# A two-layer vision tower on one core: token weights, the routing table, class tokens and the output in another form

## What is computed

```python
# layer 0: 8 experts of width 768, top 2, gelu
top_p, top_i = jax.lax.top_k(jax.nn.softmax(x @ w_gate), 2)
h = jax.nn.gelu(take(h_all, top_i), approximate=True)   # h_all = x @ w_fc, by expert
o = sum over the 2 chosen of (h @ w_proj[expert]) * top_p / sum(top_p)
# layer 1: 16 experts, 8 of width 128 and 8 of width 256, top 8
```

## Time and profile before

| | |
|---|---|
| median of three runs | 331.63 us |
| the profiled execution | 332.05 us |
| its span, first to last instruction | 329.9 us |
| TensorE busy | 290.9 us, 88% |
| VectorE busy | 263.9 us, 80% |
| ScalarE busy | 211.1 us, 64% |
| mean granted TensorE clock | 0.938 |

### The profile page before, as it was taken

The page is one execution under the profiler, slowest core; times in us unless marked ns, Lnnn a source line. Parts: engine busy times, 40 slices in busy tenths (PEclk is TensorE's granted clock), DMA queues, the critical chain, the costliest instruction groups (busy, mean ns, idle before and its releaser), DMA issues.

```text
span 329.9 us, 6328 instructions
## 1 busy us (share of the span) xinstructions
PE 290.9 (88%) x2375; PEld 264.4 (80%) x2375; DVE 263.9 (80%) x782; ACT 211.1 (64%) x519; POOL 13.7 (4%) x38
## 2 busy tenths in 40 slices
PE   8989999999999999999979126199797999999994
PEld 6979769999999999999958014178575599999993
DVE  0347778999998989998877899889859779999962
ACT  1055477777686667777658398787051788888860
POOL 0340000000000000000010002300000000000000
PEclk9999999999999999999999555589969999999999
DMA  7990403503150504020000000002300026433402
GB/s 238 284 315 25 169 3 93 207 0 150 52 200 2 201 0 170 5 108 0 2 1 3 0 0 2 0 0 87 138 2 0 2 72 209 147 124 126 118 3 50
DMA packets 10542, 27.29 MB, mean 83 GB/s; under 512 B 1352, under 2 KB 2184, under 8 KB 10512
## 3 DMA queue, kind: packets, MB, share of 16 engines
q1 hardware_dynamic: 9776, 26.01, 23.8%
q0 software_dynamic: 416, 0.68, 0.7%
q10 hardware_dynamic: 320, 0.20, 0.3%
HBM read 26.43 MB, written 0.45 MB: 81 GB/s over the span
## 4 chain that ended last, share of the span: by engine, by line
DVE 40%; PE 33%; ACT 16%; issue 5%; DMA 3%; SPq 2%; DVEq 0%; ACTq 0%
PE bank L648 11%; ACT hid_hi L1114 7%; DVE hid_lo L1474 7%; PE bank L628 5%; DVE hidden_area L1469 5%; DVE fc_lo L1448 4%; DVE pj_parts L1451 4%; PE bank L717 4%; DMA score_area<-w_l_dram 3%; ACT pj_parts L1092 3%; PE bank L618 3%; PE bank L700 2%; PE bank L698 2%; PE bank L678 1%; DVE score_area L1761 1%
## 5 line engine op out<-in xcount | busy, mean ns | idle before, releaser
L1114 ACT ACTIVATE hid_hi<-hidden_area 128x260 fp32r<-128x260 f32 x144 | 56.3, 422 | 33.5 <-DVE hidden_area L1469 31.3
L648 PE MATMUL bank<-hid_hi,pj_parts 128*128 128x260 f32 x288 | 76.3, 286 | 0.1
L1474 DVE TENSOR_TENSOR hid_lo<-hidden_area,hid_hi 128x260 fp32r<-128x260 f32 x144 | 57.0, 427 | 9.7 <-ACT hid_hi L1114 0.6
L648 PEld LDWEIGHTS bank<-hid_hi,pj_parts 128*128 128x128 f32 x288 | 54.1, 188 | 1.1 <-DVE hid_lo L1474 0.5
L1107 ACT ACTIVATE hidden_area<-bank 128x260 f32<-128x260 f32 x144 | 49.0, 377 | 6.4 <-PE bank L700 5.6
L618 PE MATMUL bank<-zeros 128*128 128x260 bf16 x239 | 34.8, 300 | 8.3 <-ACT hidden_area L1259 6.4
L648 PE MATMUL bank<-xt_hi,fc_hi 128*128 128x260 f32 x144 | 41.2, 286 | 0.3
L700 PE MATMUL bank<-xt_lo,fc_lo 128*128 128x260 f32 x144 | 41.4, 288 | 0.0
L717 PE MATMUL bank<-hid_hi,pj_parts 128*128 128x260 f32 x144 | 40.7, 283 | 0.0
L648 PE MATMUL bank<-hid_lo,pj_parts 128*128 128x260 f32 x144 | 40.7, 282 | 0.0
L648 PE MATMUL bank<-xt_lo,fc_hi 128*128 128x260 f32 x144 | 40.7, 282 | 0.0
(11 more groups left out here) (297 smaller groups left out, 557.1 us busy)
## 6 DMA issues: line engine op xcount, KB each, us to landing
raw_area<-fc_dram SPq DMA_DIRECT2D x8, 768.0 KB, 4.4
raw_area<-pj_dram SPq DMA_DIRECT2D x8, 576.0 KB, 5.6
xn<-comb_dram SPq DMA_DIRECT2D x12, 260.0 KB, 3.8
raw_area<-fc_dram SPq DMA_DIRECT2D x6, 512.0 KB, 4.1
embed_area<-embed_in_dram SPq DMA_DIRECT2D x8, 352.0 KB, 6.7
hidden_area<-comb_dram SPq DMA_DIRECT2D x9, 260.0 KB, 4.0
raw_area<-pj_dram SPq DMA_DIRECT2D x6, 384.0 KB, 4.4
score_area<-w_l_dram SPq DMA_DIRECT2D x1, 576.0 KB, 10.4
```

Of the source, the lines that this page charges most:

```text
L648: mm = pe.matmul(out, lhs[a], rhs[b], start=start and n == 0, stop=stop and n == 2, skip_group_check=True)
L1114: act.activation(hid_hi[:, x % 3, tok], hid_w[:, x % 2, tok], ACT.Copy).then_inc(hid_hi_ready[y], 1)
L1474: dve.tensor_tensor(hid_lo[:, x % 3, tok], hid_w[:, x % 2, tok], hid_hi[:, x % 3, tok].bitcast(F32), ALU.subtract).then_inc(hid_lo_ready[y ...
```

## The change

- `weights` turns the broadcast column with a transpose in place of a matmul with the identity, tile by tile, and turns tile 2 whole for both halves; its readers take their 260 columns from column 4n of the bank. The broadcast in `statistics` becomes a transpose as well.
- In layer 0 the routing table is turned in an entry of its own, `("c", 0)`, behind tile 2's entry and ahead of tile 3's, in a pair of entry banks. ScalarE copies it behind tile 2's gelu. Projection 0 no longer waits for it, and SP's write to DRAM waits for the entry. Layer 1 keeps its place. `AHEAD` of load 1 falls from 3 to 2.
- In attention 1's head the tiles are turned in the order 0, 1, 4, 2, 3; high and low parts follow that order; the first group waits for tiles 0, 1 and 4 alone; 8 fillers in place of 16.
- `patches_out` writes a tile, two images from 128 partitions: tiles 0 and 2 from SP, 1 and 3 from ScalarE's queue.

```diff
+def turn_order(r):
+    return (0, 1, 4, 2, 3) if r == 2 else (0, 1, 2, 3, 4)
...
+TURNED_TILES = [(0, 1, 2), (2, 3, 4)]
...
+        if x == 2 and not ENTRIES:
+            order += [("c", 0)]
-    return order[at - 1:at + 1] if order[at - 1][0] == "w" else order[at:at + 1]
+    first = at if order[at - 1][0] == "h" else at - 1
+    return order[first:at + 1]
...
-AHEAD = {1: 3, E0 + 1: 2}
+AHEAD = {1: 2, E0 + 1: 2}
...
-def patches_out(queue, b, done):
-    lo = (b % 2) * PATCH
-    queue.dma_start(t["out"][b, 1:S, :], h[lo:lo + PATCH, b // 2, :]).then_inc(done, 16)
+def patches_out(queue, i, done):
+    queue.dma_start(t["out"][2 * i:2 * i + 2, 1:S, :], h[:, i, :]).then_inc(done, 16)
...
-        sp.wait_ge(comb_t_ready, 2 * (y + 1))
+        if y == 0:
+            sp.wait_ge(entry_out[0], 2 * ENTRIES[0].index(("c", 0)) + 2)
+        else:
+            sp.wait_ge(comb_t_done, 2)
...
             load1(turn // 2 + 1)
-    for b in (0, 1, 4, 5):
-        sp.wait_ge(h_done, 4 + b // 4)
-        patches_out(sp, b, out_done)
+    for i in (0, 2):
+        sp.wait_ge(h_done, 4 + i // 2)
+        patches_out(sp, i, out_done)
     sp.dma_start(t["out"][:, 0, :], h[0:B, 4, :]).then_inc(out_done, 16)
-    sp.wait_ge(out_done, 16 * 5)
-    sp.wait_ge(out_done_act, 16 * 4)
+    sp.wait_ge(out_done, 16 * 3)
+    sp.wait_ge(out_done_act, 16 * 2)
...
-        for i in range(NT):
+        for i in turn_order(r):
-            pe.wait_ge(done, of * (r + r // 2) + (i // 2 + 1) * (1 + r % 2))
+            at = [k for k in turn_order(r) if k % 2 == i % 2].index(i)
+            pe.wait_ge(done, of * (r + r // 2) + (at + 1) * (1 + r % 2))
...
-            e = tiles[first_tile(y, turn)].expert
-            for i in (0, 1, 2) if n == 0 else (2, 3, 4):
-                lo, hi = max(n * HALF, i * 128), min((n + 1) * HALF, i * 128 + rows(i))
-                mm = pe.matmul(out[:, lo - n * HALF:hi - n * HALF],
-                               (comb0, comb1)[y][0:rows(i), i, e:e + 1].broadcast_to([rows(i), 128]),
-                               ident[0:rows(i), lo - i * 128:hi - i * 128], start=True, stop=True)
-            return mm
+            e, at = tiles[first_tile(y, turn)].expert, 2 * 128 * n
+            for i in TURNED_TILES[n]:
+                last = pe.transpose(out[:, i * 128 - at:i * 128 - at + rows(i)],
+                                    (comb0, comb1)[y][0:rows(i), i, e:e + 1].broadcast_to([rows(i), 128]),
+                                    ident[0:rows(i), 0:rows(i)])
+            return last
...
                     pe.wait_ge(entry_out[y], 2 * k - 3 + n)
-                out, tok = PB[PAIRS[k % 2][n]][:, 0:HALF], slice(n * HALF, (n + 1) * HALF)
+                bank, tok = PB[PAIRS[k % 2][n]], slice(n * HALF, (n + 1) * HALF)
+                out = bank[:, 0:HALF]
                 if kind == "w":
-                    mm = weights(out, x, n)
+                    mm = weights(bank, x, n)
+                elif kind == "c":
+                    for i in ((0, 1), (2, 3, 4))[n]:
+                        mm = pe.transpose(bank[0:n_exp, i * 128 - 256 * n:i * 128 - 256 * n + rows(i)],
+                                          comb0[0:rows(i), i, :], ident[0:rows(i), 0:rows(i)])
...
             if x == 0:
-                pe.wait_ge(comb_t_ready, 2 * (y + 1))
+                pe.wait_ge(first_w_ready, 2 * (y + 1))
+            if x == 0 and y:
+                pe.wait_ge(comb_t_done, 2)
...
             weights(PB[SUMS[2 + n]], 0, n).then_inc(first_w_mm, 1)
-        comb_turn(y, n_exp)
+        if y:
+            comb_turn(y, n_exp)
...
-        pe.matmul(PB[7][:, 0:n], red[0:n, r:r + 1].broadcast_to([n, 128]), ident[0:n, 0:n],
-                  start=True, stop=True).then_inc(stat_b, 1)
+        pe.transpose(PB[7][:, 0:n], red[0:n, r:r + 1].broadcast_to([n, 128]), ident[0:n, 0:n]).then_inc(stat_b, 1)
...
     transpose_x(2)
-    fill(16)
-    wait_split_x(2)
+    fill(8)
             g = 2 * j + n
+            if g == 0:
+                pe.wait_ge(xhi_ready, 3 + 4)
+                pe.wait_ge(xlo_ready, 2 + 4)
+            if g == 1:
+                wait_split_x(2)
...
         if r == 2:
-            for i in (0, 2):
-                act.wait_ge(xt_mm, NT * r + i + 2)
-                for j in range(KC):
-                    act.activation(patches_of(xt_hi, j, i), turned_patches(j, i), ACT.Copy).then_inc(xhi_ready, 1)
+            for j in range(KC):
+                act.activation(patches_of(xt_hi, j, 0), turned_patches(j, 0), ACT.Copy).then_inc(xhi_ready, 1)
+            act.wait_ge(xt_mm, NT * r + 3)
+            for j in range(KC):
+                act.activation(cls_cols(xt_hi[0:DC, j, :]), turned_cls(j), ACT.Copy).then_inc(xhi_ready, 1)
             for j in range(KC):
-                act.activation(cls_cols(xt_hi[0:DC, j, :]), turned_cls(j), ACT.Copy).then_inc(xhi_ready, 1)
+                act.activation(patches_of(xt_hi, j, 2), turned_patches(j, 2), ACT.Copy).then_inc(xhi_ready, 1)
...
                 if kind == "w":
-                    act.activation(tok_w[x % 4][:, tok], src, ACT.Identity).then_inc(entry_out[y], 1)
+                    act.activation(tok_w[x % 4][:, tok], PB[PAIRS[k % 2][n]][:, 4 * n:4 * n + HALF],
+                                   ACT.Identity).then_inc(entry_out[y], 1)
+                elif kind == "c":
+                    tok = ((0, 256), (256, 520))[n]
+                    act.activation(comb_t[0:E0, tok[0]:tok[1]], PB[PAIRS[k % 2][n]][0:E0, 0:tok[1] - tok[0]],
+                                   ACT.Copy).then_inc(entry_out[y], 1)
...
                 act.wait_ge(first_w_mm, 2 * y + n + 1)
-                act.activation(tok_w[0][:, n * HALF:(n + 1) * HALF], PB[SUMS[2 + n]][:, 0:HALF],
+                act.activation(tok_w[0][:, n * HALF:(n + 1) * HALF], PB[SUMS[2 + n]][:, 4 * n:4 * n + HALF],
         hi_part(0)
-        comb_turned(y, (E0, E1)[y])
+        if y:
+            comb_turned(E1)
...
                 entry("w", tiles[x].turn)
+            if x == 2 and y == 0:
+                entry("c", 0)
-    def comb_turned(layer, n_exp):
-        act.wait_ge(comb_mm, layer + 1)
-        act.activation(comb_t[0:n_exp, 0:512], PB[2][0:n_exp, :], ACT.Copy).then_inc(comb_t_ready, 1)
-        act.activation(comb_t[0:n_exp, 512:520], PB[3][0:n_exp, 0:B], ACT.Copy).then_inc(comb_t_ready, 1)
+    def comb_turned(n_exp):
+        act.wait_ge(comb_mm, 1)
+        act.activation(comb_t[0:n_exp, 0:512], PB[2][0:n_exp, :], ACT.Copy).then_inc(comb_t_done, 1)
+        act.activation(comb_t[0:n_exp, 512:520], PB[3][0:n_exp, 0:B], ACT.Copy).then_inc(comb_t_done, 1)
...
-    for b in (2, 3, 6, 7):
-        act.wait_ge(h_done, 4 + b // 4)
-        patches_out(act, b, out_done_act)
+    for i in (1, 3):
+        act.wait_ge(h_done, 4 + i // 2)
+        patches_out(act, i, out_done_act)
...
-        for i in (0, 2, 4):
+        for i in turn_order(r):
+            if i % 2:
+                continue
...
-        for i in (0, 2):
-            dve.wait_ge(xhi_ready, 3 + i + 2)
+        def patches_lo(i):
                                   patches_of(xt_hi, j, i).bitcast(F32), ALU.subtract).then_inc(xlo_ready, 1)
-        dve.wait_ge(xhi_ready, 9)
+        dve.wait_ge(xhi_ready, 3 + 2)
+        patches_lo(0)
+        dve.wait_ge(xhi_ready, 3 + 4)
                               ALU.subtract).then_inc(xlo_ready, 1)
+        dve.wait_ge(xhi_ready, 3 + 6)
+        patches_lo(2)
```

More of the change, by code:

```diff
@@ L274, in build @@
         comb_mm = sem("comb_mm")
-        comb_t_ready = sem("comb_t_ready")
+        comb_t_done = sem("comb_t_done")
         xhi_ready = sem("xhi_ready")
@@ L652, in comb_turn @@
             def comb_turn(layer, n_exp):
-                pe.wait_ge(comb_ready, layer + 1)
                 for i in range(NT):
```

## The result

The changed kernel takes 333.98 us in the median of four runs, where the kernel before took 331.47 in four runs beside them: a ratio of 1.0081, 95% interval 1.0053 to 1.0109. It is slower, by 2.5 us; forecast were 3.5. The profiled execution lasted 334.21 us for a span of 332.2. Two things of opposite sign stand behind that. Everything up to the output became faster, by more than forecast, and the output alone gave back more than all of it.

A forecast was written before the change was run, and what follows sets the result against it. TensorE, with VectorE close behind, was taken to bound the expert layers and VectorE the attention. Gains of 0.4 + 1.2 + 0.5 + 0.8 = 2.9 us before a 9.5 us output drain gave 335.1 us, range 332.1 to 338.4.

The forecast's parts named there:

- The output: Final output DMAs: four of 128 rows cut into 2 parts on one engine pair, drain 9.5 us; chance 0.74.
- my low bound: Output drain: shortest time for 393 KB on two engines, 8.1 us, at the best stretch's 24.2 GB/s an engine.
- The price from the output's own packets: Output drain: 42 ns a packet, 260 packets for each of two engines, 10.9 us.
- Layer 0's head: First expert layer's start: VectorE loop 1.2 us sooner, less 0.54 for AHEAD and 0.25 for table copies, net 0.4 gained.
- the 0.25 of the copies: Layer 0, tile 2: ScalarE's routing table copies cost 0.65 us, 0.41 of it idle there, so 0.25 remains.
- Attention 1's head: Projections after reordered class tokens and half the filler: VectorE's ranges start 0.5 us sooner (bounds 0.2 and 0.6).
- layer 1's head: Second expert layer's start: two pairs of token weights turned in one pass, 1.2 us gained (bounds 0.6 and 1.6).
- Statistics: Four broadcasts that VectorE waits for each lose one of two passes: 0.8 us gained (bounds 0.4 and 0.8).
- sixteen parts: Output DMAs: spread over 16 engines by their 128 source rows, giving 327.5 us; chance 0.14.
- own pairs: Output DMAs: two parts, but each queue has its own engine pair, 330.4 to 332.0 us; chance 0.06.
- two passes: Token weights and broadcasts: transposing a broadcast column still takes two passes, giving 337.0 us; chance 0.04.
- the clock in the projections: Attention 1: shorter filler lets TensorE's clock fall to 1.2 GHz before 48 projection matmuls, +5, 340 us; chance 0.02.

The follow-up runs named there:

- the mixed run: Changed kernel with SP's two tiles still written two images a DMA, but ScalarE's queue by image (four DMAs of 64 rows): 330.46 us, ratio 0.9976.

## Why the prediction was right, and where its sizes were off

**The output** decided the sign, and its step held in each link: the parts by outermost size, two of them, the packets at 260 and 276, the same pair of engines for both queues. The size: the tail was put at 1.0 + 9.5 + 0.9 = 11.4 us and was 11.9, with data from 321.5 to 331.4 us. What I had not seen is in the windows: from 322 to 324 us the two engines moved only 18 to 31 GB/s, and 46 from 325 on. Steady, 393 KB at 46 GB/s are 8.5 us, near my low bound, which came from the best stretch of the kernel at 24.2 GB/s for an engine; it was 23. The price from the output's own packets, 10.9 us, was too dear: its 42 ns a packet compare with 33 at the steady rate (23 GB/s in rows of 768 B). The 9.5, chosen between bounds of 8.1 and 12.9, came near the 9.9 that the data took, but partly by luck: the steady rate alone gives 8.5, and the rest is the slow start that I had not priced. Why the first three microseconds are slow no run here takes apart.

The Trainium skill, DMA: Bandwidth & Descriptors, in Why a DMA increments its semaphore by 16 and not by 1, gives the engine count as the largest up to 16 that divides the slowest sizes of both sides as the instruction carries them, and the lowest-numbered engines. The runs agree in the counts: 2 against 128 gave 2, 4 against 124 gave 4, 64 and 128 gave 16. They don't tell a common divisor from the smaller of the two sizes. Two queues met at one pair, but no trace here numbers the engines.

**Layer 0's head**, 0.76 for 0.4. The sum was 1.2 - 0.54 - 0.25. The first term was 1.25 at tile 1 and the second 0.54 by tile 5. The term that was wrong is the 0.25 of the copies: it was 0, so the loop stood at 0.71. Behind that stands what I had overlooked. The sum lets the VectorE loop set the pace to the end, while I had written myself that two loops run at nearly the same pace, and the loop's steps without projection pieces, 2.14 and 1.60 us, are shorter than TensorE's 2.40. At tiles 7 to 10 ScalarE waits for TensorE in the changed kernel, and a larger lead of the loop is cut to TensorE's own, as the kernel with AHEAD at 3 shows. TensorE's gain is the 0.78 of a pair turned in one pass, and the layer ends 0.76 sooner. The wait of tile 3's entry that I named is there, 0.20 us at 52.52, and costs nothing.

**Attention 1's head**, 0.52 for 0.5, and **layer 1's head**, 1.29 for 1.2 within 0.6 to 1.6: as reasoned, the latter with nearly both pairs whole.

**Statistics**, 1.48 for 0.8. The passes are worth 0.97: two at the lower clock 0.32 each and two at the higher 0.16 to 0.17, where I had halved the pair of weight loads to 0.245 and 0.145. A pair's row isn't twice a single load: one load takes 0.17 and 0.13 here, and what goes is 0.49 - 0.17 = 0.32 and 0.29 - 0.13 = 0.16. My upper bound was too low. The other 0.5 is TensorE's clock in the output projection, and that the changed kernel's profile was without the spell may be luck. I had looked for a low spell only where the change made TensorE idle, not for one in the kernel before that another execution might be without. The prediction says that the clock fell there only in the stretch of the earlier trace rows; it fell a second time in the same trace, between 236 and 238 us, with TensorE busy for 1.86 of those two microseconds, after a stretch of two in which it was busy for 0.57.

**The sum** of the gains ahead of the output, 2.9 forecast, was 4.05 by the ledger (0.76 + 0.52 + 1.48 + 1.29), and 0.57 of start that belongs to no edit came on top. Less 0.5 of a longer tail, that is the 1.2 us by which the forecast span of 333.4 lay above the 332.2. So the forecast of the whole, 3.5 us slower for 2.5, was right in sign and path; its two misses, 1.15 us of gains and 0.5 of tail, partly offset each other. The rivals: sixteen parts are refuted by the packets, own pairs by the share and the mixed run, two passes by x6 for x12, and the clock in the projections stayed at 1.00 until the window of 180 us.

## What to carry to other kernels

Before two DMAs are made one, write down both sides' sizes after joining what is contiguous: where the smaller of the two outermost sizes was below 16, it was the number of engines in every run here, and one tile for two images can take the spread from 16 to 2. If that happens, put a long dimension outermost; that gave both the spread and the saved issues, 326.41 us. And where two loops share a pace, a gain at the head is worth what the loop wins of it that sets the pace at the end, whatever the other does.

## What the hardware showed that I had not expected

- Neighbouring rows are joined before a DMA is cut: 4 x 16 and 2 x 32 neighbouring rows had 80 packets a DMA like 64 rows, 4 x 31 rows with gaps had 128 for 124 rows.
- The start varies by 1.5 us between executions of the same first instructions (routing of layer 0 at 44.74 to 46.23 us), more than any head edit of this change brings. Distances between marks repeat to 0.06 us in the expert layers.
- TensorE's second low spell (granted clock 0.50) moves: it began between 236 and 238 us in one profile and between 244 and 246 in another of the same code in that stretch, and was absent in four of fourteen.
- 128 rows into one contiguous run had a tail of 3.18 us, the two-image form with rows outermost 3.97, with the same packets. Two neighbouring writes of 768 B lie 100 KB apart in the latter; that this is the reason wasn't tried. SP's two issues also took 1.10 us there for 1.39.
